# Attention with an added bias and a layer norm: input pieces made in other graphs, a transfer issued earlier, one group of transposes ahead of the scores, and GpSimd's bias add ahead of its scaling

## What is computed

```
q, k = x @ Wq.T, x @ Wk.T
v = x @ Wv.T + bv
a = einsum(q, k) * SCALE + adj          # one adj (128 x 128) for all heads of a graph
pad_mask = all(a == 0, axis=-1)         # such a row becomes zero
p = nan_to_num(softmax(where(pad_mask, -inf, a)))
y = einsum(p, v) @ Wo.T + bo
out = layernorm(x + y)
```

## Time and profile before

| what | value |
|---|---|
| median of 3 runs | 1276.09 us (1274.07 to 1276.71) |
| the profiled execution | 1274.01 us, its span 1272.2 us |
| granted clock of TensorE | 0.995 of full speed |
| PE busy | 1225.0 us, 96% of the span |
| DVE busy | 1039.1 us, 82% |
| ACT busy | 1022.4 us, 80% |
| POOL busy | 859.3 us, 68% |
| DMA | 88.85 MB, mean 70 GB/s |

### The profile page before, as it was taken

One profiled execution on the slowest core, in us unless ns is written; L12 is line 12 of the kernel. 1 busy time (PEld: TensorE's weight loads), 2 busy tenths in 40 slices (PEclk: granted clock), 3 DMA queues, 4 the chain that ended last, 5 costly groups with the idle time before them and its releaser, 6 DMA issues.

```text
span 1272.2 us, 34265 instructions
## 1 busy us (share of the span) xinstructions
PE 1225.0 (96%) x11742; PEld 1053.9 (83%) x11742; DVE 1039.1 (82%) x5094; ACT 1022.4 (80%) x4007; POOL 859.3 (68%) x775
## 2 busy tenths in 40 slices
PE   8999999999999999999999999999999999999986
PEld 7888888888888888888888888888888888888875
DVE  5778888888888788888888887888888888878886
ACT  6877888878788778888887887788887878877874
POOL 1766767667667667676676676676766766766675
PEclk9999999999999999999999999999999999999998
DMA  6022112222122221122221222211222202222100
GB/s 228 22 70 84 61 46 84 78 70 78 34 79 78 70 84 59 47 84 78 70 78 34 79 78 70 84 63 43 84 78 70 78 32 80 79 70 84 47 26 32
DMA packets 58895, 88.85 MB, mean 70 GB/s; under 512 B 3680, under 2 KB 54624, under 8 KB 58720
## 3 DMA queue, kind: packets, MB, share of 16 engines
q1 hardware_dynamic: 58720, 86.65, 20.2%
HBM read 61.47 MB, written 25.17 MB: 68 GB/s over the span
## 4 chain that ended last, share of the span: by engine, by line
PE 70%; DVE 24%; issue 3%; POOL 2%; ACT 1%; DMA 0%; DVEq 0%; POOLq 0%; SPq 0%
PE turn_bank L211 16%; PE turn_bank L213 16%; PE turn_bank L212 16%; PE pT_bank L248 9%; PE score_bank L235 7%; PE turn_bank L260 6%; DVE neg_a L511 6%; DVE out_sb L575 3%; DVE xT_lo L487 3%; DVE stats L560 3%; DVE y_sb L555 3%; DVE neg_sum L523 2%; POOL inv_std L661 1%; DVE v_sb L501 1%; DVE mean_var L564 1%
## 5 line engine op out<-in xcount | busy, mean ns | idle before, releaser
L396 ACT ACTIVATE probs<-neg_a,neg_max 128x128 f32<-128x128 f32 x1536 | 596.6, 398 | 1.9 <-DVE neg_max L511 1.9
L654 POOL TENSOR_TENSOR probs<-probs,row_scale 128x768 f32<-128x768 f32 x256 | 376.6, 1471 | 191.7 <-DVE row_scale L539 191.7
L647 POOL TENSOR_TENSOR fold<-neg_a 128x384 f32<-128x384 f32 x256 | 271.8, 1062 | 168.6 <-DVE neg_max L511 168.6
L511 DVE CUSTOM_DVE_ANT_0 neg_a<-score_bank,adj_sb 128x128 f32<-128x128 f32 x1536 | 333.2, 285 | 0.2
L403 ACT ACTIVATE pT<-pT_bank 128x384 f32<-128x384 f32 x512 | 220.8, 485 | 103.4 <-PE pT_bank L248 103.3
L396 ACT ACTIVATION_READ_ACCUMULATOR probs<-neg_a,neg_max 128x1 f32 x1536 | 302.8, 197 | 0.0
L211 PE MATMUL turn_bank<-xT_hi,w_hi 128*128 128x512 f32 x576 | 241.0, 418 | 29.4 <-DVE xT_lo L487 27.6
L213 PE MATMUL turn_bank<-xT_hi,w_lo 128*128 128x512 f32 x576 | 227.7, 395 | 0.0
L212 PE MATMUL turn_bank<-xT_lo,w_hi 128*128 128x512 f32 x576 | 227.6, 395 | 0.0
L248 PE MATMUL pT_bank<-ident,probs 128*128 128x128 f32 x1536 | 217.3, 278 | 0.3 <-ACT pT L403 0.3
L389 ACT ACTIVATE qkT<-turn_bank 128x512 f32<-128x512 f32 x192 | 113.7, 592 | 100.2 <-PE turn_bank L213 96.8
(11 more groups left out here) (38 smaller groups left out, 2021.9 us busy)
## 6 DMA issues: line engine op xcount, KB each, us to landing
xT_raw<-xT_dram SPq DMA_DIRECT2D x32, 768.0 KB, 6.3
x_sb<-x_dram SPq DMA_DIRECT2D x32, 768.0 KB, 5.2
out_dram<-out_sb SPq DMA_DIRECT2D x128, 192.0 KB, 1.9
adj_sb<-adj_dram SPq DMA_DIRECT2D x32, 256.0 KB, 3.0
w_raw<-wq_t_dram SPq DMA_DIRECT2D x1, 576.0 KB, 5.7
w_raw<-wk_t_dram SPq DMA_DIRECT2D x1, 576.0 KB, 6.8
w_raw<-wv_t_dram SPq DMA_DIRECT2D x1, 576.0 KB, 7.8
w_raw<-wo_t_dram SPq DMA_DIRECT2D x1, 576.0 KB, 8.4
```

What stands on the lines that cost most here:

```text
L396: last = nc.scalar.activation(probs[b % 2][:, u, :], neg_a[b % 2][:, u, :], ACT.Exp, bias=neg_max[b % 2][:, u:u + 1], scale=-1.0, accum_ou ...
L511: last = nc.vector.tensor_tensor_reduce(out=neg_a[b % 2][:, u, :], in0=score_bank[trio][:, c * N:(c + 1) * N], in1=adj_sb[p][:, b, :], sca ...
L647: nc.gpsimd.tensor_tensor(fold[:, u, :], neg_a[b % 2][:, u, 0:N // 2], neg_a[b % 2][:, u, N // 2:N], ALU.add).then_inc(fold_done, 1)
L654: nc.gpsimd.tensor_tensor(probs[b % 2][:, u, :], probs[b % 2][:, u, :], row_scale[:, u].unsqueeze(2).broadcast_to([P, HALF, N]), ALU.mult) ...
```

## The change

Five edits, which the diff shows whole:

- SP: load_xT is issued one quad earlier, before the last output store of quad q for quad q + 3; the one for quad 2 goes ahead of the loop.
- PE, graph 2: transposes (3, 0) before the scores of the next quad's graph 0 and the waits for q/k and for neg_a that stand before them.
- ACT: keep_xT_hi piece 1 in graph 0 instead of graph 1, piece 2 in graph 1 instead of graph 2, after the q/k copy 4.
- DVE: keep_xT_lo piece 1 in graph 1, after add_eps; piece 2 stays in graph 2, but ahead of mean_variance and add_eps.
- POOL, every graph: add_bo after the folds, ahead of scale_half 0 and inverse_std.

```diff
--- before.py
+++ after.py
@@ -181,14 +181,16 @@
             load_xT(1)
             load_x(0, 0)
             load_x(QUAD, 1)
+            sp.wait_ge(xT_lo_done, 2 * CHUNKS)
+            load_xT(2)
 
             def quad(j, p, has_next, has_after):
                 q = 2 * j + p
 
-                if has_after:
-                    sp.wait_ge(xT_lo_done, CHUNKS * q + 2 * CHUNKS)
-                    load_xT(q + 2)
                 for b in range(QUAD):
+                    if b == 3 and q + 3 < QUADS:
+                        sp.wait_ge(xT_lo_done, CHUNKS * q + 3 * CHUNKS)
+                        load_xT(q + 3)
                     sp.wait_ge(out_done, QUAD * q + b + 1)
                     sp.dma_start(out[bass.ds(QUAD * q + b, 1), :, :].rearrange("b n f -> n (b f)"),
                                  out_sb[:, b, :]).then_inc(out_stored[b], 16)
@@ -306,11 +308,11 @@
 
                 pe.wait_ge(y_read, QUAD * q + 3)
                 attend(j, p, 2)
+                transpose_probs(j, p, 3, 0)
                 if has_next:
                     pe.wait_ge(qk_done, QK * q + 2 * QK)
                     pe.wait_ge(neg_a_done, 16 * q + 16)
                     scores(*nxt, 0)
-                transpose_probs(j, p, 3, 0)
                 if has_next:
                     project_v(*nxt, 0, 0)
                 project_out(j, p, 2)
@@ -430,7 +432,7 @@
                     keep_qk(*nxt, 4, turn)
                 if b == 3 and has_after:
                     keep_qk(*aft, 1, turn)
-                if b == 2 and has_after:
+                if b == 1 and has_after:
                     keep_xT_hi(*aft, 2)
                 if more2:
                     exp_trio(*later(j, p, b, 2), 2)
@@ -442,12 +444,11 @@
                 if b == 0 and has_after:
                     act.wait_ge(v_psum, QUAD * (2 * j + p) + QUAD)
                     keep_xT_hi(*aft, 0)
+                    keep_xT_hi(*aft, 1)
                 if b == 1 and has_next:
                     keep_qk(*nxt, 5, turn)
                 if b == 3 and has_after:
                     keep_qk(*aft, 2, turn)
-                if b == 1 and has_after:
-                    keep_xT_hi(*aft, 1)
 
             def quad(j, p, has_next, has_after):
                 for b in range(QUAD):
@@ -593,11 +594,12 @@
                     mask_half(*later(j, p, b, 2), 0)
                 residual(j, p, b)
                 statistics(j, p, b)
+                if b == 2 and has_after:
+                    keep_xT_lo(*aft, 2)
                 mean_variance(j, p, b)
                 add_eps(j, p, b)
-                if b == 2 and has_after:
+                if b == 1 and has_after:
                     keep_xT_lo(*aft, 1)
-                    keep_xT_lo(*aft, 2)
                 if b == 0:
                     keep_v(j, p, 3, turn)
                 if b == 2 and has_next:
@@ -666,10 +668,11 @@
                 if more2:
                     fold_half(*later(j, p, b, 2), 0)
                     fold_half(*later(j, p, b, 2), 1)
+                if b + 1 < QUAD or has_next:
+                    add_bo(*later(j, p, b, 1))
+                if more2:
                     scale_half(*later(j, p, b, 2), 0)
                 inverse_std(j, p, b)
-                if b + 1 < QUAD or has_next:
-                    add_bo(*later(j, p, b, 1))
                 if more2:
                     scale_half(*later(j, p, b, 2), 1)
```

## The result

| | before | after |
|---|---|---|
| median | 1275.09 us (4 runs) | 1296.01 us (4 runs, 1295.85 to 1298.9) |
| profiled execution, span | 1274.01, 1272.2 | 1295.85, 1294.0 |
| PE busy | 1225.0 | 1230.7 |
| DVE busy | 1039.1 | 1079.9 |
| distance of the last xT_lo's end in graph 2 from attend(1) | 17.69 | 18.42 |

The change makes the kernel slower: ratio 1.0168, 95% interval 1.0149 to 1.0188. It lies in the steady part: 30 quads lose 0.73 us each, 21.9 us, and the span grew by 21.8.

What follows compares the result with a forecast made beforehand. PE's order was taken as the bound, with a 0.91 us hole a quad waiting for xT_lo. 30 x 0.56 = +16.8 us on 1274.01 gave 1290.8, a median of 1292; range 1275 to 1301, the forecast's own 1286 to 1299.

Steps and rivals of the forecast that it cites:

- The transfer and ScalarE at nothing: Earlier load_xT and ScalarE's moved xT_hi pieces: both covered, costing nothing; uncovered, at most 6.3 us once and 0.5 a quad.
- The scores' delay, +0.41: Graph 2: scores begin 0.63 to 0.81 us later behind the transposes, so bias_trio starts 0.41 later in DVE's chain.
- PE does the same work: PE, graph 2: transposes and scores only change places, so PE's work stays the same.
- Graph 1's delay of 0.38: DVE would leave graph 1 0.38 us late; this and the scores' 0.41 cover each other, so 0.41 counts once.
- row_scale held for the whole add, residual +1.27: Graph 2: row_scale waits for POOL's whole 1.00 us add_bo, so residual starts 1.27 us later, scores' 0.41 included.
- xT_lo(2) held by the scaling, ending 0.53 after it: Graph 2: scale_half 0 holds DVE's xT_lo(2) until 569.71; it ends 0.53 us later, at 570.24.
- The sum: PE starts after xT_lo 0.56 us later a quad, bounds +0.36 and +0.72; 30 quads give +16.8 us.
- The hole as all that can be won, 0.91: PE's wait for xT_lo, 0.91 us in a quad, is all the change can win in its steady part.
- POOL's wait for row_scale shrinks: A sign that the forecast is right: POOL waits less for DVE's row_scale; no size given.
- the one that row_scale slips in first: Rival: residual on time, but add and scaling run to about 569.85 and hold xT_lo(2); +0.7 a quad, 1296, chance 0.12.
- the one that only the add holds: Rival: row_scale waits for the add, but xT_lo(2) runs beside the scaling; +0.36 a quad, 1286, chance 0.15.
- the faster one: Rival: two-input DVE work is not held behind POOL in graph 2; -0.51 a quad, 1260, or 1248; chance 0.15.

Runs made afterwards that it cites:

- the pieces alone: Only the input pieces and their transfer moved, PE's and POOL's orders as before the change, against the kernel before: 1265.23 us, ratio 0.9931.
- pe_back: The changed kernel with PE's old order in graph 2 put back (scores, then transposes): 1284.70 us, ratio 1.0075 to the kernel before.
- the test with epsilon first: The changed kernel with mean_variance and add_eps put ahead of xT_lo(2) again: 1295.87 us, against 1296.01.
- the kernel without it: The kernel before with early transfer, all xT_hi in graph 0, xT_lo pieces earlier, xT_lo(2) before residual in graph 2: 1239.26 us, ratio 0.9733.

## Why the prediction was right

The direction and the range were right, and so was the mechanism: 1292 forecast, 1296.01 measured, a loss of 20.9 us for a forecast of 16 (30 x 0.56 = 16.8 against the profiled execution, whose span grew by 21.8). By its steps:

- *The transfer and ScalarE at nothing:* right for the changed kernel. ACT waits for xT_raw twice (4.7 us) where it waited 14 times (9.4 us), and PE never does. The late q/k copy is covered only by the swap: with PE's old order it costs PE 0.30 a quad, as the pieces alone show.
- *The scores' delay, +0.41:* the step that was too small. I took the first result at the scores' slot, 0.88 after their start. It is 573.39 - 572.32 = 1.07 after it; the scores' start, 0.81 later than before, was right. The biases are 0.56 late, here and in the kernel with PE's order alone.
- *"PE does the same work":* wrong by 0.18 us a quad (2.48 against 2.30). In the changed kernel the hole swallows it, so the time did not show it; the wait, 1.44, looks like the forecast 1.5 because of it: the hole would be 0.18 longer if PE had come to it as early as before. That the wait came out as forecast is luck.
- *Graph 1's delay of 0.38 covers the scores' 0.41:* not quite; the moved xT_lo(1), and row_scale and inv_std held in that graph, bring 0.22 (pe_back: 11.27 against 11.05), so the other 0.34 of the biases' 0.56 is the swap's, and 11 us came back with PE's old order.
- *row_scale held for the whole add, residual +1.27:* +1.33, of which 0.56 is the scores and 0.77 the add; the add's term had been 0.86. Small as it is, row_scale does not slip in. The reading that out_sb starts 0.07 after the add in every graph holds for graphs 1 and 3; in graphs 0 and 2 it starts 0.37 and 0.61 after it, and is held for what is left.
- *xT_lo(2) held by the scaling, ending 0.53 after it:* 0.56, and the test with epsilon first shows that it is holding. This was seen by only 0.16 us in the trace before. The rule cited from the Trainium skill (SBUF — State Buffer, section "Who interferes with whom"), that whoever issues first has the pair for the whole instruction, agrees with these runs both ways: row_scale's 0.92 us here, and the scaling's 1.85 where xT_lo came first.
- *The sum:* 0.73 a quad for 0.56. Since xT_lo(2) is held until the scaling ends, it is the scaling's delay that counts: forecast 0.41 + 0.77 = 1.18, measured 1.32, and xT_lo(2) ends 0.03 later behind it than forecast. The scores' 0.15 is most of the difference. The first hole comes 1.05 us late, 0.73 of it its own quad's, and what follows the last hole got 0.3 shorter, inside the bounds of the tail.
- *The hole as all that can be won, 0.91:* wrong. It was worth 1.18, as the kernel without it shows.
- *POOL's wait for row_scale shrinks:* hardly, 189.5 us for 191.7. In graph 1 of the quad it falls from 0.30 to 0.10 ahead of half 0, and rises from 1.16 to 1.46 ahead of half 1.

The time alone would not have told the forecast from its rivals: the one that row_scale slips in first had 1296. It is refuted by row_scale's 0.92 us, the one that only the add holds by xT_lo's 1.12, and the faster one by both.

## What to carry to other kernels

Moving an instruction of GpSimd moves what it holds on VectorE: before such a move, list the VectorE instructions with two SBUF inputs (and those like the normalise, a tensor_scalar from SBUF to SBUF, 0.48 us alone and 1.15 beside the add) that will run beside it in the new place, and look for the one on the critical chain, however few elements it has. Where two such instructions must meet, put the critical one ahead: 0.15 and 0.17 us were enough here, and the scaling behind it took 1.85 us instead of 1.47. A hole that shrinks is not yet time won: look whether the engine comes to it later. When several edits come together, put each back alone: here one lost 22 us, one 11, and the rest, which was the idea, gained 9. These do not add up to the 20.9, and need not: alone in the kernel before, the same two edits lost 25 and 17, since delays of several edits cover each other.

## What was not expected of the hardware

- An idle row of PE understates its hole: 0.91 us in the row, 1.18 in the quad. 0.17 of it is that the row counts from the modelled end of the last product, 0.34 after its start, where the next product would start 0.17 after it; 0.10 is the longer first product.
- The same 24 score matmuls and 6 transposes take 1.51 us in one order and 1.69 in the other (the earlier trace rows and the rows above); it shows only where PE has no hole.
- An instruction that already waits for POOL's fold gets through ahead of POOL's next. In graph 1 of the changed kernel the fold ends at 567.80 and the add's row begins at 567.76. live, which takes 0.17 where nothing holds it, takes 0.40 and ends at 567.82; row_scale, 0.09 after the add's start, has to wait for its end. It is read from these rows; no run tests it.

```profile
567.42 0.40 DVE L534 TENSOR_TENSOR live<-neg_max,neg_sum 128x6 f32<-128x6 f32 x1
567.85 0.93 DVE L540 TENSOR_TENSOR row_scale<-live,inv_sum 128x6 f32<-128x6 f32 x1
```

```profile
566.40 1.40 POOL L649 TENSOR_TENSOR fold<-neg_a 128x384 f32<-128x384 f32 x1 [0.25 <-DVE neg_max L512]
567.76 1.00 POOL L642 TENSOR_TENSOR x_sb<-x_sb,bo_sb 128x384 f32<-128x384 f32 x1
```
